# First stage of an attention and expert kernel rewritten as one list of 128 steps

## The chip, the cores and the metric

The kernel runs on one core of one Trainium2 chip. Its time is the device time of one launch in microseconds (us). The core has five engines that run their own instruction lists in order and meet only at semaphores: TensorE (PE, with PEld for its weight loads), VectorE (DVE), ScalarE (ACT), GpSimd (POOL) and SyncE (SP), which here only issues DMA transfers. ACT also issues a few transfers.

## What is computed

There are 16 batches of 128 rows by 256 columns in float32. Four residual blocks follow one another:

```
x = x + cross_attention_8_heads(layernorm(x), ctx, ctx)   # attention over the 256 columns, 16 rows a head
x = x + expert_choice_ffn(layernorm(x))                   # y = layernorm(x) @ expert_w + expert_b, router logits @ router_w + router_b
x = x + masked_cross_attention(layernorm(x), ctx)
x = x + top_half_ffn(layernorm(x))                        # 64 of 128 rows a batch through a gelu layer
```

The change touches the first stage, which does the first block and, of the second, the product `y` and the router's logits. For each of 16 batches and 8 heads it forms scores of 256 by 256, subtracts each row's maximum, exponentiates, multiplies by the values, divides, adds to `x`, normalizes and multiplies by `[expert_w | router_w]` (272 columns).

## The kernel before

**Steps.** One head of one batch is a step: 128 steps, numbered 8 b + (place of the head), 16 to a unit of two batches. A step has two products on PE. `scores` (L1089) gives the scores for the row maxima, which DVE takes with `maximum` (L527). `scores_t` (L1099) gives the transposed scores with the negated maxima added by two extra rows of the contraction; ACT exponentiates them (`exponential`, L891). Every fourth step `values` (L1112) multiplies four heads' probabilities by the values. `scores` runs 16 steps ahead of the exponentials at first and, catching up by two a step in steps 8 to 15, 24 ahead from step 16 on: there step t has `scores` and `maximum` number t + 24, `scores_t` number t + 2 and `exponential` number t. There are two banks for the scores and two for the transposed scores, so each producer may be two ahead of its consumer.

**Stacks.** Both products read a stack: the context and the normalized `x` of a unit, each as three bfloat16 parts (high, middle, low). For unit w the chain is: the unit is loaded (`load_stage`, L222); ACT makes the high part (`high_k`, L914), POOL the rest (`rest_k`, L334), ACT the middle (`mid_k`), POOL the low part (`low_k`, L339); DVE normalizes `x` (`stats_q`, `scale_q`) and `high_q`, `rest_q`, `mid_q`, `low_q` (L343 to 350) do the same for it; SP writes the six parts to DRAM (L233 to 243), issues the load of the next unit, waits for the parts and issues nine loads of the stack (`load_stacks`, L245). PE may start `scores` of unit w (step 12 for unit 2, step 16 w - 24 for later ones) once `stacks_loaded` has counted them. `mid_q` of unit 3 stands in step 13, of later units in step 16 w - 42 or 16 w - 44.

**Batch work.** After its eight steps a batch goes through `take_even` (ACT, L932: two products that pick the even heads), `gather_parts` (DVE, L539: two instructions of 256 columns), `invert` (reciprocal), `bring_over` (shuffle and product), `add_x1` (sum with `xs`, then the statistics), `root_rows` (POOL: inverse root), `scale_rows`, a transposition (PE), `take_xnt` (ACT), `yw` (PE, L1147) and `take_yw` (DVE, L576: bias added to `y` and to the logits). The row maxima of a batch are transposed (`max_t`), negated in two parts (`neg_high` on ACT, `neg_low` on DVE) and sent into the stack by two small DMAs (`send_neg_max`, L903).

**Order.** Each engine's order is written out by hand: a function `unit` for each engine with a place j for every piece, called once a unit, of which units 2 and 3 run in a hardware loop (`Fori`). On DVE `maximum` comes first in its step. On ACT `mid_k` stands right behind the first exponential of a unit. On POOL `rest_k` of the next stack is the last piece of a unit, behind `root_rows` of that unit's even batch; for the odd batch `root_rows` stands in the next unit.

After the stage come a softmax of the logits, a search of thresholds on DVE and PE, and a second pipeline over batch pairs that does the rest.

## Time and profile before

| what | value |
|---|---|
| three runs | 427.8, 426.61, 420.42 us; median 426.61 |
| profiled execution | 422.43 us, of which the span from first to last instruction 420.2 us |
| mean granted TensorE clock | 0.841 |
| busy, share of the span | PE 279.6 us (67%), DVE 317.7 (76%), ACT 167.6 (40%), POOL 94.8 (23%) |
| first exponential | 44.3 us from the start of the span |
| last exponential | starts at 237.5 us |
| first instruction of PE after the stage | 253.2 us |

The span begins with the first instruction. The stage ends at 253.2 us, where PE transposes the softmax of the logits; the remaining 167 us are the search and the second pipeline. A granted clock of 1.00 is TensorE at 2.4 GHz, and 0.5 is 1.2 GHz; values between are means over a stretch.

### The profile page before, as it was taken

To read this page: it belongs to the slowest core of one execution; us is meant where nothing else is said; L and a number is where in the kernel's file an instruction comes from. 1 tells how busy PE (TensorE), PEld (TensorE's weight loads), DVE (VectorE), ACT (ScalarE), POOL (GpSimd) and SP (SyncE) were. 2 spreads that over 40 slices of the span, in tenths; PEclk is the share of its full clock that TensorE was granted. 3 is DMA by queue.
4 is the path that set the end of the run, shared out by engine and by line. 5 is a ranking of instruction groups with operands and counts; after the bars stand their busy time and mean duration, and the time that the engine had idled before them with its cause. 6 is when DMAs were issued, how large, how long until landed. Compare 5 with 4: busy or idle time off the path is not lost.

```text
span 420.2 us, 7370 instructions
## 1 busy us (share of the span) xinstructions
PE 279.6 (67%) x1872; PEld 182.5 (43%) x1872; DVE 317.7 (76%) x989; ACT 167.6 (40%) x397; POOL 94.8 (23%) x222
## 2 busy tenths in 40 slices
PE   1134777777886877877778621001559999999996
PEld 0011333353442544444334310000438988888884
DVE  5847458899989889799986748888377888787631
ACT  4110543464654536464556500000111566445631
POOL 1101323352415224111111110000133322333200
PEclk9999975789698886899989965555555999999999
DMA  2789388959294581740000380000000000000001
GB/s 88 202 189 153 98 221 187 166 150 165 71 197 79 145 126 54 146 80 1 2 1 2 100 301 0 1 0 2 1 0 0 2 25 25 25 0 25 26 27 51
DMA packets 24379, 32.90 MB, mean 78 GB/s; under 512 B 4066, under 2 KB 22434, under 8 KB 22818
## 3 DMA queue, kind: packets, MB, share of 16 engines
q1 hardware_dynamic: 23842, 32.48, 33.5%
q10 hardware_dynamic: 512, 0.13, 0.2%
q8 instruction: 10, 0.16, 0.2%
q14 instruction: 15, 0.12, 0.1%
HBM read 24.02 MB, written 8.39 MB: 77 GB/s over the span
## 4 chain that ended last, share of the span: by engine, by line
DVE 35%; PE 33%; issue 12%; DMA 8%; ACT 4%; POOL 3%; SPq 2%; DVEq 1%; ACTq 1%; POOLq 0%
DVE row_max L531 7%; PE t_bank L1355 5%; PE pv_bank L1273 5%; PE pv_bank L1121 4%; DMA q_stack<-q_parts_dram 4%; DVE denom_inv L549 3%; PE score_bank L1094 3%; PE scoret_bank L1107 3%; PE t_bank L1150 2%; PE score_bank L1336 2%; DMA q_parts_dram<-q_parts 2%; ACT probs L895 2%; DMA q_stack<-neg_max 2%; PE score_bank L1303 2%; DVE junk L705 1%
## 5 line engine op out<-in xcount | busy, mean ns | idle before, releaser
L895 ACT ACTIVATE probs<-scoret_bank 128x512 f32<-128x512 f32 x128 | 73.1, 596 | 52.5 <-PE scoret_bank L1107 42.3
L531 DVE TENSOR_REDUCE row_max<-score_bank 128x2 f32<-128x512 f32 x112 | 74.4, 679 | 24.3 <-PE score_bank L1094 23.1
L1107 PE MATMUL scoret_bank<-q_stack,k_stack 98*128 98x256 bf16 (+1 forms) x256 | 54.6, 301 | 28.1 <-ACT probs L895 18.7
L1094 PE MATMUL score_bank<-k_stack,q_stack 96*128 96x256 bf16 (+1 forms) x240 | 53.6, 314 | 19.1 <-DMA q_stack<-q_parts_dram 11.0
L355 POOL TENSOR_SCALAR var_eps<-mv 128x1 f32<-128x1 f32 x48 | 9.2, 192 | 189.5 <-DVE mv L567 106.9
L1107 PEld LDWEIGHTS scoret_bank<-q_stack,k_stack 98*128 98x128 bf16 (+1 forms) x256 | 24.2, 104 | 46.6 <-ACT probs L895 20.5
L1121 PE MATMUL pv_bank<-probs,values_ones 128*32 128x256 f32 x512 | 42.0, 455 | 1.0 <-ACT probs L895 1.0
L1094 PEld LDWEIGHTS score_bank<-k_stack,q_stack 96*128 96x128 bf16 (+1 forms) x240 | 21.7, 105 | 47.8 <-issue 15.3
L1273 PE MATMUL pv_bank<-q_stack,k_stack 128*128 (+1 forms) x256 | 36.0, 285 | 0.4 <-ACT q_stack L1070 0.4
L1045 ACT COPY xnt<-score_bank 128x256 f32<-128x256 f32 x16 | 6.0, 373 | 74.6 <-PE score_bank L1294 74.6
L1273 PEld LDWEIGHTS pv_bank<-q_stack,k_stack 128*128 128x128 f32 x256 | 33.9, 202 | 1.3 <-issue 0.9
L1355 PE MATMUL t_bank<-k_stack,probs 128*128 128x256 f32 x128 | 29.4, 382 | 0.0
L357 POOL TENSOR_TENSOR rstd<-var_eps,minus_half 128x1 f32<-128x1 f32 x48 | 26.1, 543 | 8.8 <-POOL var_eps L355 8.8
L549 DVE RECIPROCAL denom_inv<-denom 128x256 f32<-128x256 f32 x16 | 27.7, 1732 | 0.0
L1355 PEld LDWEIGHTS t_bank<-k_stack,probs 128*128 128x128 f32 x128 | 23.7, 190 | 2.9
L1254 PE MATMUL t_bank<-count,same_expert 128*128 128x3 bf16 x15 | 2.8, 187 | 31.4 <-DVE equal L705 31.4
L1150 PE MATMUL t_bank<-wr_moving,xnt 128*128 128x272 f32 x64 | 22.0, 474 | 1.2 <-ACT xnt L943 1.2
L1064 ACT ACTIVATE probs<-pv_bank,b1s 128x128 f32<-128x128 f32 x64 | 17.6, 379 | 11.8 <-PE pv_bank L1273 11.7
L1121 PEld LDWEIGHTS pv_bank<-probs,values_ones 128*32 128x32 f32 x512 | 15.0, 122 | 16.2 <-issue 9.0
L1144 PE MATMUL t_bank<-ident,xn 128*128 128x128 f32 x32 | 7.0, 303 | 18.5 <-DVE xn L573 10.2
L1137 PE MATMUL t_bank<-ident,ctx_stage 128*128 128x128 f32 x32 | 7.6, 383 | 16.3 <-DMA x_stage<-in_x_dram 16.3
L1150 PEld LDWEIGHTS t_bank<-wr_moving,xnt 128*128 128x128 f32 x64 | 13.4, 234 | 8.1 <-issue 4.1
(182 smaller groups left out, 534.5 us busy)
## 6 DMA issues: line engine op xcount, KB each, us to landing
q_stack<-q_parts_dram SPq DMA_DIRECT2D x48, 128.0 KB, 6.9
k_parts_dram<-k_parts SPq DMA_DIRECT2D x24, 128.0 KB
q_parts_dram<-q_parts SPq DMA_DIRECT2D x24, 128.0 KB
k_stack<-k_parts_dram SPq DMA_DIRECT2D x8, 384.0 KB, 4.6
ctx_stage<-in_ctx_dram SPq DMA_DIRECT2D x8, 256.0 KB, 3.2
x_stage<-in_x_dram SPq DMA_DIRECT2D x8, 256.0 KB, 3.9
k_stack<-k_parts_dram SPq DMA_DIRECT2D x8, 256.0 KB, 5.3
xs<-in_x_dram SPq DMA_DIRECT2D x8, 256.0 KB, 7.3
```

The costliest lines, as they stand in the source:

```text
L355: pool.tensor_scalar(work, variance, EPS, factor, ALU.add, ALU.mult).then_inc(s[summed], 1)
L357: pool.tensor_tensor(dst, work, minus_half[:, 0:dst.shape[1]], ALU.pow).then_inc(s[ready], 1)
L531: dve.tensor_reduce(row_max[:, i, :, h], score_bank[bank_of][:, :].rearrange("p (m n) -> p m n", m=2), AX.X, ALU.max).then_inc(s["max_done ...
L549: dve.reciprocal(denom_inv[:, i, :], denom[:, i, :]).then_inc(s["div_step"], 1)
L895: act.activation(probs[:, j % PROBS, :], scoret_bank[j % 2][:, :], ACT.Exp).then_inc(s["exp_done"], 1)
L1064: act.activation(hid[:, h, :], hid_bank[h // 4][:, (h % 4) * P:(h % 4 + 1) * P], ACT.Gelu_apprx_tanh, bias=b1s[:, h:h + 1]).then_inc(s["f_ ...
L1094: ins = pe.matmul(to[:, m * D:(m + 1) * D], q_stack[0:QROWS, slot, h, b_in, m * P:(m + 1) * P], k_stack[0:QROWS, slot, h, b_in, :], start= ...
L1107: ins = pe.matmul(scoret_bank[j % 2][:, k * D:(k + 1) * D], k_stack[0:SROWS, slot, h, b_in, k * P:(k + 1) * P], q_stack[0:SROWS, slot, h, ...
L1121: ins = pe.matmul(pv_bank[i][pair * Q:(pair + 1) * Q, odd * D:(odd + 1) * D], values_ones[:, i, k, pair, odd, :], probs[:, (j - GROUP + 1 ...
L1150: ins = pe.matmul(t1_bank[:, 0:D + NE], xnt[:, i, k, :], wr_moving[:, k, :], start=(k == 0), stop=(k == 1))
L1273: ins = pe.matmul(hid_bank[h // 4][:, (h % 4) * P:(h % 4 + 1) * P], w1s[:, k, h * P:(h + 1) * P], zg[:, k, bass.ds(P * t, P)], start=(k == ...
L1355: ins = pe.matmul(y_bank[:, 0:D], hid[:, h, :], w2s[:, h, :], start=(h == 0), stop=(h == NF - 1))
```

## The change

The four `unit` functions and the loops go. Each engine runs one unrolled loop over t = 0 to 151, and tables say in which step each piece of a stack or of the maxima stands. `scores`, `scores_t` and `exponential` keep their places. The pieces of a batch b now stand at fixed steps: `values` 8b+7, `take_even` 8b+10, `gather_parts` 8b+11, `invert` 8b+12, `bring_over` 8b+13, `add_x1` 8b+14, `stats_x1` 8b+16, `root_rows` 8b+17, `scale_rows` 8b+18, transposition 8b+20, `take_xnt` 8b+21, `yw` 8b+22, `take_yw` 8b+24. `mid_k` stands three steps behind `high_k`.

Moved to other engines or merged: the sum `add_x1` goes from DVE to POOL; the statistics stay on DVE. The biases become three bfloat16 rows, made once on POOL (`split_bias`, ten small instructions), and are added by a third matmul in `yw`; `take_yw` is then one copy of 272 columns on ACT. `gather_parts` is one instruction of 512 columns. Some buffers of the second pipeline now lie in the stacks' memory, and `y` and `logits` share one tensor with rows of 272. The diff, cut to what is spoken of:

```
+def ahead(t):
+
+    if t < NH:
+        return [STEPS + t]
+    if t < STEPS:
+        return [2 * t + NH, 2 * t + NH + 1]
+    return [t + STEPS + NH] if t + STEPS + NH < LAST else []
...
+MAX_T = {1: 1, 2: 9, 3: 15, **{b: NH * b - 13 for b in range(4, NB)}}
+STAGE = {3: 9, 4: 21, **{w: STEPS * (w - 3) for w in range(5, NU)}}
+MID_K = {2: 0, 3: 11, 4: 23, **{w: STAGE[w] + 3 for w in range(5, NU)}}
+SCALE_Q = {2: 1, 3: 11, 4: 24, **{w: STAGE[w] + 6 for w in range(5, NU)}}
+HIGH_Q = {2: 3, 3: 13, 4: 25, **{w: STAGE[w] + 7 for w in range(5, NU)}}
+MID_Q = {2: 5, 3: 15, 4: 27, **{w: STAGE[w] + 9 for w in range(5, NU)}}
+CTX_T = {2: 5, 3: 12, 4: 23, **{w: STAGE[w] + 7 for w in range(5, NU)}}
+TAKE_VT = {2: 7, 3: 13, 4: 25, **{w: STAGE[w] + 9 for w in range(5, NU)}}
...
-        num_low = sb("num_low", [P, 2, D])
-        sum_high = sb("sum_high", [P, 2, D])
-        numer = sb("numer", [P, 2, D])
-        denom = sb("denom", [P, 2, D])
+        low_part = sb("low_part", [P, 2, 2, D])
+        gathered = sb("gathered", [P, 2, 2, D])
...
+            def add_x1(b, u, i, first):
+                wait_apart(pool, s["div_step"], 4 * b + 4)
+                wait_apart(pool, s["x_loaded"], 16 * (u + 1))
+                if not first:
+                    wait_apart(pool, s["xn_ready"], b - 1)
+                    wait_apart(pool, s["kept"], b - 1)
+                pool.tensor_tensor(x_new[:, i, :], gathered[:, i, 1, :], xs[:, b, :], ALU.add).then_inc(s["x1_done"], 1)
...
+                step(pool.tensor_copy(bias_terms[:, 0, :], bias_f[:, :]))
+                step(pool.tensor_tensor(bias_left[:, 0, :], bias_f[:, :], bias_terms[:, 0, :], ALU.subtract))
+                step(pool.tensor_copy(bias_terms[:, 1, :], bias_left[:, 0, :]))
+                step(pool.tensor_tensor(bias_left[:, 1, :], bias_left[:, 0, :], bias_terms[:, 1, :], ALU.subtract))
+                step(pool.tensor_copy(bias_terms[:, 2, :], bias_left[:, 1, :]))
+                for part in range(3):
+                    wait_apart(pool, s["ident_done"], 1)
+                    ins = pool.tensor_scalar(bias_kept[:, part, :], bias_terms[:, part, :], ident[0:3, part:part + 1], None, ALU.mult)
+                step(ins)
+                step(pool.tensor_tensor(bias_sum[:, :], bias_kept[:, 0, :], bias_kept[:, 1, :], ALU.add))
+                pool.tensor_tensor(bias_parts[:, :], bias_sum[:, :], bias_kept[:, 2, :], ALU.add).then_inc(s["bias_done"], 1)
...
+            for t in range(LAST + 3 * NH):
+                for b in range(NB):
+                    if t == NH * b + 17:
+                        root_rows(b, b % 2)
+                        keep_rows(x_new, b, b % 2)
+                for w in due(STAGE, t - 1):
+                    rest_k(w)
+                for w in due(STAGE, t - 2):
+                    root_q(w)
+                for w in due(MID_K, t - 1):
+                    low_k(w)
+                for w in due(HIGH_Q, t - 1):
+                    rest_q(w)
+                for w in due(MID_Q, t - 1):
+                    low_q(w)
+                for b in range(1, NB):
+                    if t == max(NH * b - 5, 2):
+                        fill_values(b, b // 2, b % 2, b < 2)
+                if t == NH + 1:
+                    split_bias()
+                for b in range(NB):
+                    if t == NH * b + 14:
+                        add_x1(b, b // 2, b % 2, b < 2)
...
                 dve.wait_ge(s["even_taken"], b + 1)
-                dve.scalar_tensor_tensor(denom[:, i, :], odd_heads, low[:, 0:1], sum_high[:, i, :],
+                if not (isinstance(b, int) and b < 2):
+                    dve.wait_ge(s["x1_done"], b - 1)
+                dve.scalar_tensor_tensor(gathered[:, i].rearrange("p k n -> p (k n)"), pv_bank[i][:, :], high[:, 0:1],
+                                         low_part[:, i].rearrange("p k n -> p (k n)"),
                                          ALU.mult, ALU.add).then_inc(s["div_step"], 1)
-                dve.scalar_tensor_tensor(numer[:, i, :], odd_heads, high[:, 0:1], num_low[:, i, :],
-                                         ALU.mult, ALU.add).then_inc(s["div_step"], 1)
 
...
+                                  ALU.mult).then_inc(s["div_step"], 1)
+
...
-                dve.tensor_tensor(y[:, b, :], t1_bank[:, 0:D], eb_rows[:, 0:D], ALU.add)
-                dve.tensor_tensor(logits[:, b, :], t1_bank[:, D:D + NE], eb_rows[:, D:D + NE], ALU.add).then_inc(s["yw_done"], 1)
...
+                    for b in range(NB):
+                        i = b % 2
+                        if t == NH * b + 16:
+                            stats_x1(b, i)
+                        if t == NH * b + 18:
+                            scale_rows(b, i, b < 2)
+                        if t == NH * b + 11:
+                            gather_parts(b, i)
+                        if t == NH * b + 12:
+                            invert(b, i)
+                        if t == NH * b + 13:
+                            bring_over(b, i)
+                    for w in due(STAGE, t if t < STEPS * 2 else t - 1):
+                        stats_q(w)
+                    for w in due(SCALE_Q, t):
+                        scale_q(w)
+                    for b in due(MAX_T, t - 2):
+                        neg_low(b, b % 2)
 
...
+            def take_yw(b):
+                act.wait_ge(s["yw_ready"], b + 1)
+                act.copy(y_ext[:, b, :], t1_bank[:, 0:D + NE]).then_inc(s["yw_done"], 1)
...
+                act.mul(low_part[:, i, 0, :], pv_bank[i][:, D:2 * D], low[:, 0:1])
+                act.mul(low_part[:, i, 1, :], pv_bank[i][:, 0:D], low[:, 0:1]).then_inc(s["even_taken"], 1)
...
+            for t in range(LAST + 3 * NH + 2):
+                if t < LAST:
+                    exponential(t // STEPS, t % STEPS, t < STEPS)
+                for b in range(NB):
+                    i = b % 2
+                    if t == NH * b + 24:
+                        take_yw(b)
+                    if t == NH * b + 10:
+                        take_even(b, i, b < 2)
+                    if t == NH * b + 21:
+                        take_xnt(b, i, b < 2)
+                for b in due(MAX_T, t - 1):
+                    neg_high(b, b // 2, b % 2)
+                for b in due(MAX_T, t - 3):
+                    send_neg_max(b // 2, b % 2)
+                for w in due(STAGE, t):
+                    high_k(w)
+                for w in due(MID_K, t):
+                    mid_k(w)
+                for w in due(HIGH_Q, t):
+                    high_q(w)
+                for w in due(TAKE_VT, t):
+                    take_vt(w)
+                for w in due(MID_Q, t):
+                    mid_q(w)
 
...
-                    ins = pe.matmul(t1_bank[:, 0:D + NE], xnt[:, i, k, :], wr_moving[:, k, :],
-                                    start=(k == 0), stop=(k == 1))
+                    pe.matmul(t1_bank[:, 0:D + NE], xnt[:, i, k, :], wr_moving[:, k, :],
+                              start=(k == 0), stop=False)
+                ins = pe.matmul(t1_bank[:, 0:D + NE], ones_bf[0:3, 0:P], bias_parts[:, :], start=False, stop=True)
...
+                for n in (ahead(t) if t < LAST else []):
+                    if n % STEPS == 0:
+                        pe.wait_ge(s["stacks_loaded"], 144 * (n // STEPS + 1))
+                    scores(score_bank[n % 2], n // STEPS, (n % STEPS) // NH, HEADS[n % NH], n - 1)
+                if t + 2 < LAST:
+                    scores_t(t + 2, (t + 2) // STEPS, (t + 2) % STEPS, True)
+                for b in due(MAX_T, t):
+                    pe.wait_ge(s["neg_done"], b)
+                    pe.wait_ge(s["vt_done"], before(CTX_T, t))
+                    max_t(b, b % 2)
+                for w in due(CTX_T, t):
+                    pe.wait_ge(s["neg_done"], before(MAX_T, t))
+                    ctx_t(w)
+                if t < LAST and t % GROUP == GROUP - 1:
+                    values(t, t // NH, t % STEPS, t < STEPS)
+                for b in range(NB):
+                    if t == NH * b + 20:
+                        if b > 0:
+                            pe.wait_ge(s["yw_done"], b)
+                        xn_t(b, b % 2)
+                    if t == NH * b + 22:
+                        if b == 0:
+                            pe.wait_ge(s["bias_done"], 1)
+                        yw(b, b % 2)
```

## Rows read from the trace of the kernel before

**Rows 1.** Busy time by stretch: start and end, length, engines, granted clock, DMA share, GB/s.
```profile
77.00:99.00 22.00, 17.36 (x140) 10.04 (x132) 19.20 (x41) 14.26 (x31) 7.79 (x13) 0.89 0.77 159
91.10:170.40 79.30, 60.85 (x444) 33.53 (x444) 71.20 (x145) 41.69 (x87) 25.97 (x49) 0.85 0.59 123
170.40:193.60 23.20, 18.18 (x146) 9.72 (x144) 20.42 (x42) 12.18 (x27) 3.17 (x11) 0.93 0.50 92
193.60:214.30 20.70, 15.38 (x141) 8.67 (x141) 19.31 (x41) 10.73 (x22) 2.38 (x8) 1.00 0.01 2
214.30:237.50 23.20, 17.40 (x148) 8.92 (x144) 16.72 (x40) 14.85 (x32) 4.15 (x12) 0.93 0.01 2
237.50:253.20 15.70, 5.50 (x28) 2.75 (x28) 8.55 (x30) 2.44 (x7) 2.16 (x6) 0.76 0.79 267
```

**Rows 2.** Who waited for whom between 99 and 180 us: total us, times, longest.
```profile
ACT k_parts L922 <- POOL k_rest L336: 10.7, 3, 3.8
```

**Rows 3.** Timeline around the start of unit 3: start, us, engine, line, operation, tiles, idle before.
```profile
127.86 1.15 POOL L336 TENSOR_TENSOR k_rest<-ctx_stage,k_parts 128x512 f32<-128x512 f32 x1
127.98 1.18 DVE L573 TENSOR_SCALAR xn<-x_new,mv,rstd 128x256 f32<-128x256 f32 x1
129.04 0.62 ACT L922 CAST k_parts<-k_rest 128x512 bf16<-128x512 f32 x1 [3.43 <-POOL k_rest L336]
```

**Rows 4.** Timeline of DVE and POOL, batch work in the last units.
```profile
207.61 0.46 DVE L542 SCALAR_TENSOR_TENSOR denom<-pv_bank,low,sum_high 128x256 f32<-128x256 f32 x1
208.39 0.67 DVE L531 TENSOR_REDUCE row_max<-score_bank 128x2 f32<-128x512 f32 x1
208.99 1.73 DVE L549 RECIPROCAL denom_inv<-denom 128x256 f32<-128x256 f32 x1
212.60 0.41 DVE L563 TENSOR_TENSOR x_new<-numer,xs 128x256 f32<-128x256 f32 x1
213.05 0.43 DVE L565 BATCH_NORM_STATS2 st<-x_new 128x6 f32<-128x256 f32 x1
214.01 0.19 POOL L355 TENSOR_SCALAR var_eps<-mv 128x1 f32<-128x1 f32 x1 [8.66 <-DVE mv L567]
214.88 0.40 POOL L366 COPY xs<-x_new 128x256 f32<-128x256 f32 x1
232.24 0.42 DVE L580 TENSOR_TENSOR y<-t_bank,eb_rows 128x256 f32<-128x256 f32 x1
232.66 0.47 DVE L542 SCALAR_TENSOR_TENSOR denom<-pv_bank,low,sum_high 128x256 f32<-128x256 f32 x1
```

**Rows 5.** Timeline of the chain that makes a stack: units 2 and 3, then 5.
```profile
51.16 1.16 POOL L350 TENSOR_TENSOR q_parts<-q_rest,q_parts 128x512 bf16<-128x512 f32 x1 [1.84 <-ACT q_parts L930]
...
66.67 0.62 ACT L930 CAST q_parts<-q_rest 128x512 bf16<-128x512 f32 x1
68.89 1.04 PE L1094 MATMUL score_bank<-k_stack,q_stack 96*128 96x256 bf16 x4 [2.15 <-DMA q_stack<-q_parts_dram]
69.61 1.29 DVE L531 TENSOR_REDUCE row_max<-score_bank 128x2 f32<-128x512 f32 x2 [1.61 <-PE score_bank L1094]
70.38 0.60 ACT L895 ACTIVATE probs<-scoret_bank 128x512 f32<-128x512 f32 x1 [3.10 <-PE scoret_bank L1107]
...
137.10 1.16 POOL L350 TENSOR_TENSOR q_parts<-q_rest,q_parts 128x512 bf16<-128x512 f32 x1 [1.57 <-ACT q_parts L930]
145.19 2.95 SPq L261 DMA_DIRECT2D q_stack<-q_parts_dram  x6
```

**Rows 6.** The page's list of DMA issues: KB each, median us from issue to landing.
```profile
q_stack<-q_parts_dram SPq DMA_DIRECT2D x48, 128.0 KB, 6.9
```

**Rows 7.** Timeline of ACT near the end of the stage, and its copy by line.
```profile
222.35 2.17 ACT L895 ACTIVATE probs<-scoret_bank 128x512 f32<-128x512 f32 x4 [2.13 <-PE scoret_bank L1107]
...
236.96 1.08 ACT L895 ACTIVATE probs<-scoret_bank 128x512 f32<-128x512 f32 x2 [1.74 <-PE scoret_bank L1107]
L943 ACT COPY xnt<-t_bank 128x256 f32<-128x256 f32 x16 | 5.6, 353 | 7.6 <-PE t_bank L1144 7.6
```

More of the change, by code:

```diff
@@ L38, with due, before @@
 PROBS = 2 * GROUP
-LEAD = NH
+LAST = STEPS * NU
+def ahead(t):
[12 more added lines that the diff above has]
+TAKE_VT = {2: 7, 3: 13, 4: 25, **{w: STAGE[w] + 9 for w in range(5, NU)}}
+def due(table, t):
+    return [n for n in sorted(table) if table[n] == t]
+def before(table, t):
+    return min(table) + sum(1 for n in table if table[n] < t)
 def build_program(nc, x, ctx_2048, mask, router_w, router_b, expert_w, expert_b,
@@ L304, in unit @@
                     load_stacks(u + 3, reused)
-            unit(0, True, True, False)
-            with sp.Fori(1, NU - 4) as u:
-                unit(u, True, True, True)
-            unit(NU - 4, False, True, True)
-            unit(NU - 3, False, False, True)
-            unit(NU - 2, False, False, True)
+            for u in range(NU - 1):
+                unit(u, u < NU - 4, u < NU - 3, u > 0)
             sp.wait_ge(s["scorest_ready"], STEPS * NU)
@@ L381, in _ @@
             root_q(2)
-            low_k(2)
-            rest_q(2)
-            low_q(2)
-            def unit(u, first, second, parts, more_parts, last):
-                if second:
-                    rest_k(u + 3)
-                    root_q(u + 3)
-                if parts and not first:
-                    low_k(u + 3)
-                    rest_q(u + 3)
-                fill_values(2 * u + 1, u, 1, first)
-                if parts and not first:
-                    low_q(u + 3)
-                if not first:
-                    root_rows(2 * u - 1, 1)
-                    keep_rows(x_new, 2 * u - 1, 1)
-                if first:
-                    rest_k(u + 3)
-                    root_q(u + 3)
-                if not last:
-                    fill_values(2 * u + 2, u + 1, 0, False)
-                if first:
-                    low_k(u + 3)
-                    rest_q(u + 3)
-                    low_q(u + 3)
-                root_rows(2 * u, 0)
-                keep_rows(x_new, 2 * u, 0)
-                if more_parts and not first:
-                    rest_k(u + 4)
-                    root_q(u + 4)
@@ L992, in unit @@
-            def unit(u, second, last, parts, more_parts):
-                for j in range(STEPS):
-                    exponential(u, j, False)
-                    if j == 1:
-                        take_even(2 * u - 1, 1, second)
-                    if j == 1 and second:
-                        high_k(u + 3)
-                    if j == 2 and not last:
-                        neg_high(2 * u + 2, u + 1, 0)
-                    if j == 3 and not last:
-                        send_neg_max(u + 1, 0)
-                    if j == (3 if second else 0) and parts:
-                        mid_k(u + 3)
-                    if j == 2:
-                        take_xnt(2 * u - 2, 0, second)
-                    if j == (4 if second else 2) and parts:
-                        high_q(u + 3)
-                    if j == (6 if second else 4) and parts:
-                        mid_q(u + 3)
-                    if j == 6 and parts:
-                        take_vt(u + 3)
-                    if j == 9:
-                        take_even(2 * u, 0, False)
-                    if j == 10 and not last:
-                        neg_high(2 * u + 3, u + 1, 1)
-                    if j == 11 and not last:
-                        send_neg_max(u + 1, 1)
-                    if j == 10:
-                        take_xnt(2 * u - 1, 1, second)
-                    if j == 13 and more_parts:
-                        high_k(u + 4)
```

284 lines of the change are left out of this document (47 added, 237 removed).

## The prediction

> **What bounds the kernel now.** I read first the totals: DVE is the busiest engine (317.7 us), yet 76% is a mean over unlike parts, so it proves little. The table of busy time by stretch comes next, with cuts where DVE starts the maximum of steps 48, 96 and 112, ends the last one, where the last exponential starts, and where the stage ends at 253.2 us [rows 1]. The reader is to see three regimes. From 193.6 to 214.3 us DVE is busy 19.31 of 20.7 us at a granted clock of 1.00: 16 steps bound by DVE. From 91.1 to 170.4 us the same 16 steps take 26.4 us (79.3 over 3), though DVE's work is only 23.7 a stretch: something else stops it. After 214.3 us there are no maxima, and a chain through all engines sets the pace.
>
> The waits name the something: ACT's `mid_k` stood 3 times for `rest_k` of POOL, 10.7 us together [rows 2]. The timeline shows how: ACT idles 3.43 us with 15 exponentials queued behind it, while POOL, which had stood behind an inverse root, makes `rest_k` from 127.86 us on, and a DVE instruction that normally takes 0.41 us takes 1.18 beside it [rows 3].
>
> **DVE's work.** Start to start, the sum costs 0.45 us (212.60 to 213.05), the two bias additions 0.42 (232.24 to 232.66), the two gathers 0.78 (207.61 to 208.39) [rows 4]. The merged gather of 512 columns is not in the trace: at least the 0.60 of a maximum over 512 columns in the same memory (208.39 to 208.99), at most the two halves, 0.78. I take the middle, 0.69, as it has one more operand than the maximum. So 0.45 + 0.42 + 0.09 = 0.96 us go for each batch, 1.9 us per 16 steps. A stretch with no new stack falls from 20.7 to 18.8 us. One with a stack took 22.0 where little stalled (77 to 99 us [rows 1]); less 1.9 that is 20.1.
>
> **What is added elsewhere.** POOL's sum: between the 0.40 us of a 256-column copy [rows 4] and the 1.15 of a 512-column subtraction [rows 3], and I take 0.58, half the latter, as it reads two inputs. POOL was busy 26.0 of 79.3 us, so 1.2 us a stretch lie beside DVE; they matter only through what queues behind: `low_q` and `root_rows`. ACT's copy of 272 columns is 0.37 us by the 353 ns of the 256-column one [rows 7]; ACT is busy 41.7 of 79.3 us and it costs nothing but once at the end. The third matmul of `yw` is at most a half of a score's pair, which takes 1.04 us for four at half clock [rows 5], so 0.26 us; PE has 20.7 - 15.4 us to spare. The ten bias instructions on POOL stand at step 9, in a pause where it waits for unit 3's data; if each cost 0.4 to 1.15 us and the cover went, that would be 4 to 11 us of delay for `rest_k` of unit 3. I take none, since unit 3 is late for another reason, next.
>
> **The chain that takes the stall's place.** What is late next is the stack itself. From the end of POOL's `low_q` (52.32) to PE's first product from stack 2 (68.89) it was 16.6 us; for stack 5 from 138.26 to the last issue at about 147.6, and 6.9 us to land, 16.3 [rows 5, 6]. Below 16 nothing excludes a gain but the queue's order is unchanged; above, more overlap with other transfers may cost. I take 17, with 16 and 20 as ends. The diff moves `mid_q` of unit 3 from step 13 to step 15, and this crosses a barrier: exponential 13 ran before stack 2 had landed, but exponential 14 starts at 70.38, after it [rows 5], since step 12 of PE needs stack 2. Worked out for stack 3: stack 2 lands at 69.4, half a microsecond later than before because its own `mid_q` moves one step; DVE's first two maxima end at 71.3; the reciprocal, now in step 12 behind them, ends at 73.0 (1.73 less overlap [rows 4]); two maxima, then shuffle and product end at 75.1; POOL's sum stands ahead of `low_q` and ends at 76.0; `low_q` ends at 77.1. Before, `mid_q` was at 66.67 [rows 5] and `low_q` ended by 68.6. So stack 3 lands at 77.1 + 17 = 94.1 and the maximum of step 48 starts at 94.8 (0.72 us later, as 68.89 to 69.61 [rows 5]), 3.7 us behind the 91.1 of before.
>
> For stack 4, `scale_q` stands in the very step that waits for stack 3, then `high_q`, `rest_q`, `mid_q`, `low_q`: about 5.9 us, so step 64 comes 5.9 + 17 = 22.9 us later, at 117.7. For later stacks `low_q` follows stack w by 0.72 (product) + 0.6 (maximum) + 0.96 (statistics to POOL, 213.05 to 214.01) + 1.27 (inverse root and copy, 214.01 to 215.28) [rows 4] + 1.15 (itself) = 4.7 us. The loop's period is 21.7 us, against 20.1 of DVE. With DVE's small waits and collisions I take 22 for each of the next three.
>
> **The sum.** Step 112's maximum: 117.7 + 3 x 22 = 183.7 (193.6 before). Last one: + 18.8 = 202.5 (214.3). Last exponential: 24 steps at (236.96 - 222.35) / 16 = 0.91 us [rows 7], 21.9 us, so 224.4 (237.5). End of the stage: the 15.7 us of before and 0.5 for the two new hand-overs and the third matmul: 240.6 (253.2). Gain 12.6 us; the second pipeline keeps its length. Against the profiled execution, 422.4 - 12.6 = 409.8; its time lies 1% under the median of 426.6, from which I get **414.0**.
>
> **The rivals.** *The stack is never late.* If the loads come sooner, or DVE's other work hides them, step 48 stays at 91.1, four stretches of 20.1 follow, then 18.8, 21.9 and 16.2: 228.4, a gain of 24.8, **401.8**. For it: the list of waits shows none of PE for a stack after the one of 68.89 [rows 5]. Against: `mid_q` of unit w had 18 to 20 steps to spare, and has 13 to 15 now, 16.3 to 18.8 us at the new pace of 20.1 / 16.
>
> *The chain is longer.* At 20 us step 48 comes at 97.8, step 64 25.9 later, and three periods of 24.7 end at 197.8; with 18.8, 21.9 and 16.2 the stage ends at 254.7: **428**, no change. For it: unit 5's issues on SP fill 9.9 of its 16.3 us (138.26 to 148.14 [rows 5]), and the next unit's load goes ahead of the stack's.
>
> *POOL blocks DVE.* The 1.18 in place of 0.41 us [rows 3] is a DVE instruction that ended with POOL's, not after its own time. Should each of 16 sums stop DVE for its whole 0.58, 9.3 us are lost: **423**. The Trainium skill (SBUF — State Buffer, section "SBUF: two separate sides") says that a POOL instruction and a DVE one with two SBUF inputs or in a two-port mode exclude each other for a whole instruction; by it, moving work from DVE to POOL may return nothing, which is this case; the trace agrees where the two meet. Against: in the step of the sum DVE mostly reduces scores, and in rows 3 the meeting was with an instruction twice as long.
>
> *Slower: TensorE's clock.* PE's work in a stretch with a stack is 60.85 / 3 x 0.85 = 17.2 us at full clock [rows 1]. If PE, stopped at step 16w - 24 by each late stack, mostly runs at 1.2 GHz, it becomes the bound. It decides from a mean granted clock of 0.70, where 17.2 / 0.70 = 24.6 us undo the gain. At 0.65 four stretches of 26.5 from 94.8, then 23.7, 21.9 and 16.2 end at 262.6: **436**. For it: the stretches with stalls have 0.85, the ones without 0.93 to 1.00. Against: the stalls of 3.43 us vanish, the new ones are about 1 to 3 us. The Trainium skill (TensorE: Matmul & The Clock Gate, section "HAM oscillation — how this bites in real kernels") says that PE slows down again at each wait for data; by that the late stacks would cost twice.
>
> **How the numbers follow.** Chances: forecast 0.50, stack never late 0.20, longer chain 0.15, POOL blocks 0.07, clock 0.08. About 2% (8.5 us, so below 418.1) is what can be told from no change here. Faster: nine tenths of the forecast and the first rival, 0.65. Slower: 0.08. Within: the rest, 0.27. The range runs from 398 (the first rival with a few microseconds more) to 426 (most of the second); it leaves out the clock, half of the longer chain and the ends of the runs' own spread of 7 us.
>
> **What would show it.** Right: no ACT wait of `mid_k` for POOL; PE waits for the DMA of a stack at step 24 (some 6 us) and again at step 40 (1 to 3); 21 to 23 us from the maximum of step 64 to that of 80; no DVE instruction reading the product of `yw`; last exponential near 224 and stage end near 241. Wrong: the maximum of step 48 at 91 or before, stretches of 20 us, or a granted clock under 0.8 from 95 to 200 us. A second pipeline that changes its length would break the sum as well.

## Result: 6.95% slower, and the profile after

The kernel after took **453.57 us** (median of four runs, 452.29 to 454.3), the kernel before 425.75 (420.42 to 427.8). The ratio is 1.0695, with a 95% interval from 1.0591 to 1.0799. The profiled execution took 453.62 us, of which its span is 451.8. I had predicted 414.0, with a range from 398 to 426.

The page of the kernel after, its busy line and four groups (busy us, mean ns of one, idle time before, releaser):

```profile
PE 293.6 (65%) x1888; PEld 185.2 (41%) x1888; DVE 298.2 (66%) x925; ACT 170.7 (38%) x413; POOL 113.1 (25%) x248
...
L574 DVE TENSOR_REDUCE row_max<-score_bank 128x2 f32<-128x512 f32 x112 | 73.5, 675 | 65.0 <-PE score_bank L1027 64.6
L875 ACT ACTIVATE probs<-scoret_bank 128x512 f32<-128x512 f32 x128 | 74.2, 600 | 77.0 <-issue 50.8
...
L404 POOL TENSOR_TENSOR x_new<-gathered,xs 128x256 f32<-128x256 f32 x16 | 11.6, 722 | 73.4 <-DVE gathered L599 68.4
...
L586 DVE SCALAR_TENSOR_TENSOR gathered<-pv_bank,high,low_part 128x512 f32<-128x512 f32 x16 | 11.9, 742 | 6.3 <-ACT low_part L921 6.3
```

DVE lost the work it was meant to lose: 317.7 us before, 298.2 now. The maxima cost the same, yet DVE now waits 64.6 us for PE's scores ahead of them; the page of before has this for the same group:

```profile
L531 DVE TENSOR_REDUCE row_max<-score_bank 128x2 f32<-128x512 f32 x112 | 74.4, 679 | 24.3 <-PE score_bank L1094 23.1
L895 ACT ACTIVATE probs<-scoret_bank 128x512 f32<-128x512 f32 x128 | 73.1, 596 | 52.5 <-PE scoret_bank L1107 42.3
```

The exponentials changed what they wait for: PE before, "issue" (50.8 us) now, which means that ACT's own queue was held up by something that is no busy instruction. Busy time of the kernel after by stretch of sixteen exponentials (numbers 38, 54, 70, 86 and 102 start about at the cuts) is to be read beside [rows 1]:

```profile
126.00:154.40 28.40, 21.86 (x147) 11.13 (x145) 19.43 (x41) 13.98 (x31) 10.04 (x18) 0.76 0.53 112
154.40:182.00 27.60, 21.07 (x151) 10.87 (x150) 20.15 (x41) 14.28 (x32) 10.04 (x18) 0.81 0.55 116
182.00:209.00 27.00, 19.92 (x150) 10.64 (x150) 19.60 (x37) 13.34 (x30) 7.00 (x14) 0.87 0.46 98
209.00:235.00 26.00, 20.05 (x143) 10.63 (x144) 17.84 (x34) 11.18 (x26) 4.74 (x12) 0.80 0.05 12
```

The last row is the telling one. DMA is busy 5% there: no stack is made, and [rows 1] had 16 such steps in 20.7 us, bound by DVE. Now DVE is busy 17.84 of 26 us. So the loss comes also where no stack is made. The waits of 90 to 250 us (total, times, longest):

```profile
ACT probs L875 <- issue: 45.3, 11, 5.1
DVE row_max L574 <- PE score_bank L1027: 44.1, 16, 4.8
PE scoret_bank L1040 <- ACT probs L875: 36.8, 26, 2.9
```

ACT is held 11 times in some 11.5 batches, 4.1 us each. The timeline shows by what (ACTq is ACT issuing DMAs):

```profile
208.45 1.74 DVE L592 RECIPROCAL denom_inv<-gathered 128x256 f32<-128x256 f32 x1
208.56 0.60 ACT L875 ACTIVATE probs<-scoret_bank 128x512 f32<-128x512 f32 x1
...
210.66 0.43 DVE L596 STREAM_SHUFFLE denom_own<-denom_inv 128x256 f32<-128x256 f32 x1
...
211.13 0.42 DVE L599 TENSOR_TENSOR gathered<-gathered,denom_own 128x256 f32<-128x256 f32 x1
...
211.48 0.40 DVE L579 SCALAR_TENSOR_TENSOR neg_max<-t_bank,neg_max 8x256 bf16<-8x256 f32 x1
...
211.91 1.29 ACTq L886 DMA_DIRECT2D q_stack<-neg_max  x2
...
213.25 1.08 ACT L875 ACTIVATE probs<-scoret_bank 128x512 f32<-128x512 f32 x2 [4.09 <-issue]
213.90 0.39 PE L1040 MATMUL scoret_bank<-q_stack,k_stack 98*128 98x256 bf16 x2 [2.71 <-ACT probs L875]
...
215.23 0.60 PE L1027 MATMUL score_bank<-k_stack,q_stack 96*128 96x256 bf16 x2
...
215.94 0.69 DVE L574 TENSOR_REDUCE row_max<-score_bank 128x2 f32<-128x512 f32 x1 [2.86 <-PE score_bank L1027]
```

Read it from 211.48. `neg_low` starts there, the last piece of its step on DVE, behind the reciprocal, the shuffle and the product. ACT's last exponential ended at 209.16; the next piece in its queue is `send_neg_max`, which needs `neg_low`. It issues its two DMAs at 211.91, and the next exponential, whose input had long been in its bank, starts at 213.25. PE stood for the free bank until 213.90, did `values` (1.07 us) before the next scores, and DVE ran dry until 215.94. The same rows stand 14 us later, and so on: a loop DVE, ACT, PE, DVE, closed once a batch. In the kernel before `neg_low` stood right behind the maximum:

```profile
207.28 0.40 DVE L536 SCALAR_TENSOR_TENSOR neg_max<-t_bank,neg_max 8x256 bf16<-8x256 f32 x1
...
207.71 1.36 ACTq L906 DMA_DIRECT2D q_stack<-neg_max  x2
...
209.17 2.17 ACT L895 ACTIVATE probs<-scoret_bank 128x512 f32<-128x512 f32 x4 [1.60 <-PE pv_bank L1121]
```

It is ahead of the two gathers and the reciprocal [rows 4], and ACT hardly waits. In the list `neg_low` of batch b is at step 8b - 11, which is the step of another batch's `bring_over`, and stands behind it.

### The profile page after: what moved, and what is told of

It reads as the page before. It is cut to its first block, busy times and chain, and to the rows that moved or that the text cites. A ratio compares the mean times of both kernels' runs of the same rounds, so it can differ in the third digit from the quotient of the medians.

```text
span 451.8 us, 6847 instructions
## 1 busy us (share of the span) xinstructions
PE 293.6 (65%) x1888; PEld 185.2 (41%) x1888; DVE 298.2 (66%) x925; ACT 170.7 (38%) x413; POOL 113.1 (25%) x248
## 4 chain that ended last, share of the span: by engine, by line
DVE 33%; PE 33%; issue 11%; DMA 8%; ACT 5%; ACTq 4%; POOL 4%; SPq 2%; DVEq 1%; POOLq 0%
PE pv_bank L1054 7%; DVE row_max L574 6%; DVE denom_inv L592 5%; PE scoret_bank L1040 4%; ACTq L886 4%; DMA q_stack<-q_parts_dram 4%; PE t_bank L1237 4%; PE score_bank L1027 4%; PE pv_bank L1155 3%; ACT probs L875 2%; DMA q_parts_dram<-q_parts 2%; PE score_bank L1218 2%; POOL rstd L390 2%; DVE junk L685 1%; DVE denom_own L596 1%
## 5 line engine op out<-in xcount | busy, mean ns | idle before, releaser
L574 DVE TENSOR_REDUCE row_max<-score_bank 128x2 f32<-128x512 f32 x112 | 73.5, 675 | 65.0 <-PE score_bank L1027 64.6
L875 ACT ACTIVATE probs<-scoret_bank 128x512 f32<-128x512 f32 x128 | 74.2, 600 | 77.0 <-issue 50.8
L1040 PE MATMUL scoret_bank<-q_stack,k_stack 98*128 98x256 bf16 x256 | 61.1, 332 | 53.4 <-ACT probs L875 44.5
L1027 PE MATMUL score_bank<-k_stack,q_stack 96*128 96x256 bf16 x240 | 57.7, 337 | 23.3 <-DMA q_stack<-q_parts_dram 16.1
L1040 PEld LDWEIGHTS scoret_bank<-q_stack,k_stack 98*128 98x128 bf16 x256 | 24.8, 114 | 75.7 <-ACT probs L875 57.6
L1054 PE MATMUL pv_bank<-probs,values_ones 128*32 128x256 f32 x512 | 48.6, 514 | 0.0
L1027 PEld LDWEIGHTS score_bank<-k_stack,q_stack 96*128 96x128 bf16 x240 | 21.4, 114 | 56.5 <-DVE row_max L574 21.5
L404 POOL TENSOR_TENSOR x_new<-gathered,xs 128x256 f32<-128x256 f32 x16 | 11.6, 722 | 73.4 <-DVE gathered L599 68.4
L390 POOL TENSOR_TENSOR rstd<-var_eps,minus_half 128x1 f32<-128x1 f32 x48 | 26.3, 549 | 9.1 <-POOL var_eps L388 9.1
L592 DVE RECIPROCAL denom_inv<-gathered 128x256 f32<-128x256 f32 x16 | 27.9, 1744 | 0.1
L1054 PEld LDWEIGHTS pv_bank<-probs,values_ones 128*32 128x32 f32 x512 | 16.3, 133 | 19.2 <-issue 15.0
L1083 PE MATMUL t_bank<-wr_moving,xnt 128*128 128x272 f32 x64 | 18.6, 415 | 1.2 <-ACT xnt L927 1.2
L1070 PE MATMUL t_bank<-ident,ctx_stage 128*128 128x128 f32 x32 | 7.2, 367 | 16.2 <-DMA x_stage<-in_x_dram 16.2
L586 DVE SCALAR_TENSOR_TENSOR gathered<-pv_bank,high,low_part 128x512 f32<-128x512 f32 x16 | 11.9, 742 | 6.3 <-ACT low_part L921 6.3
```

Of the source, the lines that this page charges most:

```text
L390: pool.tensor_tensor(dst, work, minus_half[:, 0:dst.shape[1]], ALU.pow).then_inc(s[ready], 1)
L574: dve.tensor_reduce(row_max[:, i, :, h], score_bank[bank_of][:, :].rearrange("p (m n) -> p m n", m=2), AX.X, ALU.max).then_inc(s["max_done ...
L592: dve.reciprocal(denom_inv[:, i, :], gathered[:, i, 0, :]).then_inc(s["div_step"], 1)
L875: act.activation(probs[:, j % PROBS, :], scoret_bank[j % 2][:, :], ACT.Exp).then_inc(s["exp_done"], 1)
L1027: ins = pe.matmul(to[:, m * D:(m + 1) * D], q_stack[0:QROWS, slot, h, b_in, m * P:(m + 1) * P], k_stack[0:QROWS, slot, h, b_in, :], start= ...
L1040: ins = pe.matmul(scoret_bank[j % 2][:, k * D:(k + 1) * D], k_stack[0:SROWS, slot, h, b_in, k * P:(k + 1) * P], q_stack[0:SROWS, slot, h, ...
```

## Experiments

Theory at the outset: the place of `neg_low`. Rivals: the later pieces of the stacks; TensorE's lower clock; the work moved to POOL and ACT. The code shows the edits shortened. Ratios are to runs of the kernel before on the same chip (medians 420.74 to 422.83).

**1. Only `neg_low` moved, in the kernel after:** one step earlier and ahead of the batch pieces.

```
  # DVE, step t, behind the maximum
+    for b in due(MAX_T, t - 1):
+        if b >= 4: neg_low(b, b % 2)
  # last in the step
     for b in due(MAX_T, t - 2):
-        neg_low(b, b % 2)
+        if b < 4: neg_low(b, b % 2)
```

> The kernel after with one piece moved: for batches from 4 on, DVE's neg_low stands one step earlier, ahead of that step's statistics, reciprocal, shuffle and product instead of behind them. Theory A (order on DVE): in the kernel after, ACT's send of the maxima waits for neg_low, which queues behind a 1.66 us reciprocal, two maxima and 0.8 us of shuffle and product; ACT is stopped 4.0 us and issues for 1.3 us at each batch, and PE and then DVE run dry for 2.9 to 3.5 us. Moving it 3 us forward takes about 3 us off each of 12 batches: 415 to 422 us in place of 453.6, ACT's idle time in front of an exponential that follows a send falls from 33 us (8 times between 130 and 250 us) to under 12. Theory B (the chain of the stacks, period 4.7 + 17 us, has become the bound): no gain beyond 3 us, and PE waits for a stack's transfer grow. Theory C (TensorE at 1.2 GHz is the bound): under 5 us of gain.

Measured: 419.91 us, ratio 0.9953 (0.991 to 0.9995), against 1.0695. By the medians that is 34 us less than the kernel after, from one instruction of 0.40 us at another place. Its timeline, then its stretches (in the last two POOL makes no parts of a stack, in the last nothing is moved either):

```profile
186.96 0.40 DVE L579 SCALAR_TENSOR_TENSOR neg_max<-t_bank,neg_max 8x256 bf16<-8x256 f32 x1
187.06 0.60 ACT L879 ACTIVATE probs<-scoret_bank 128x512 f32<-128x512 f32 x1
...
187.29 1.73 DVE L592 RECIPROCAL denom_inv<-gathered 128x256 f32<-128x256 f32 x1
187.39 1.29 ACTq L890 DMA_DIRECT2D q_stack<-neg_max  x2
...
188.73 1.09 ACT L879 ACTIVATE probs<-scoret_bank 128x512 f32<-128x512 f32 x2 [1.07 <-PE scoret_bank L1044]
```
```profile
132.00:155.90 23.90, 18.68 (x151) 10.09 (x150) 21.50 (x41) 14.29 (x33) 10.06 (x18) 0.93 0.62 131
155.90:179.70 23.80, 18.56 (x151) 10.08 (x150) 21.28 (x41) 14.26 (x32) 10.07 (x18) 0.93 0.64 117
179.70:198.70 19.00, 16.58 (x149) 9.04 (x147) 18.34 (x35) 11.96 (x27) 4.77 (x12) 1.00 0.58 107
198.70:216.80 18.10, 14.28 (x132) 7.66 (x131) 16.09 (x32) 11.99 (x27) 4.77 (x12) 1.00 0.01 2
```

The reciprocal now lies beside the two DMA issues. The clock rises too: 0.93 where stacks are made against 0.76 to 0.87, 1.00 in the last stretch against 0.80. The lower clock of the kernel after came with its stops and went with them; how many of the 34 us it carried itself no run separates.

**2. The consumer moved instead:** ACT's `send_neg_max` two steps later, `neg_low` left last.

```
-for b in due(MAX_T, t - 3):
+for b in range(1, NB):
+    if t == MAX_T[b] + (3 if b < 4 else 5):
         send_neg_max(b // 2, b % 2)
```

> The kernel after with ACT's send of the negated maxima two steps later (for batches from 4 on), DVE's order untouched. Theory A (ACT's wait for DVE, not the DMA issue itself, costs): ACT reaches the send when neg_low is done, the exponentials of the next two steps run ahead, and the time falls to 415 to 430 us; the transfer has 6 steps left until PE needs it. If what costs were the 1.3 us that ACT spends on two issues, nothing would change: 450 to 455. Theory B (stacks) and C (clock): within 5 us of 453.6.

Measured: 426.85 us, ratio 1.0104 (1.0021 to 1.0187), 27 us less than the kernel after. So it isn't the time at which `neg_low` runs that costs, but what queues behind the instruction that waits for it. What keeps this kernel 7 us above experiment 1 stays open.

**3. Rival, the stacks:** their pieces back at about the steps of before, `neg_low` left last.

```
-STAGE = {3: 9, 4: 21, **{w: STEPS * (w - 3) ...}}
+STAGE = {3: 8, 4: 17, **{w: STEPS * (w - 3) - 3 ...}}
-SCALE_Q = {2: 1, 3: 11, 4: 24, **{w: STAGE[w] + 6 ...}}     # MID_K, HIGH_Q likewise
+SCALE_Q = {2: 1, 3: 10, 4: 19, **{w: STAGE[w] + 4 ...}}
-MID_Q = {2: 5, 3: 15, 4: 27, **{w: STAGE[w] + 9 ...}}
+MID_Q = {2: 5, 3: 13, 4: 23, **{w: STAGE[w] + 7 ...}}
```

> The kernel after with the stack pieces (high_k, mid_k, stats_q, scale_q, high_q, mid_q and with them POOL's four) moved back to about the steps of the kernel before, so that mid_q has 20 steps to the first product instead of 15 (17 instead of 13 for stack 4, 11 instead of 9 for stack 3). Theory B (the late stack sets the period of 28 us): gain of 10 us or more. Theory A: PE's waits for stacks vanish, but the gain is under 5 us but for the first stacks (stack 3 lands at 97.7 and stack 4 at 125.7 us: up to 8 us there), 445 to 453 us in all.

Measured: 460.42 us, ratio 1.0906 (1.0826 to 1.0986): slower still, where I had expected 445 to 453. The rival falls: here stacks 5 to 7 landed 18 to 21 us before their first maxima, in the kernel after 6.7 to 7.7 us before, so in neither were they what was late. The timeline of its first unit shows a new stall:

```profile
65.36 2.85 POOL L425 TENSOR_SCALAR bias_kept<-bias_terms,ident 3x272 bf16<-3x272 bf16 x3 [0.24 <-POOL bias_terms L422]
...
70.97 1.56 DVE L530 TENSOR_SCALAR qn<-x_stage,mv,rstd_q 128x256 f32<-128x256 f32 x2 [6.88 <-POOL rstd_q L390]
...
76.07 0.62 ACT L910 CAST q_parts<-qn 128x512 bf16<-128x512 f32 x1 [11.65 <-issue]
```

With the data of unit 3 wanted sooner, the ten bias instructions stand in front of its inverse root on POOL, DVE stops in its queue for it, and ACT's send, which waits for DVE, holds ACT for 11.65 us. This is the same mechanism with a longer cause, but it is not why the kernel is slower than the one after: the maximum of step 48 comes 1.7 us later there, that of step 64 0.7 us. The rest is lost behind it, where steps 64 to 112 take 88.8 us in place of 82.2; why stays open.

**4. The loss put into the kernel before:** `neg_low` behind `bring_over` two steps later, the send two later; nothing else of the change. (Two pieces that share a bank with the maxima, the context's transposition on PE and a copy on ACT, move by two steps and one.)

```
-if j == 2 and scored and not first:  neg_low(2 * u + 2, 0)
+if j == 4 and scored and not first:  neg_low(2 * u + 2, 0)    # last in the step
...
-if j == 3 and not last:              # ACT, the send
+if j == 5 and not last:
```

> The kernel before with the suspected order put in: from unit 1 on neg_low stands behind shuffle and product, two steps later, and ACT's send two steps later with it (the transposition of the context on PE and its copy also move 2 and 1 steps, since they share a bank). Nothing else of the change. Theory A: ACT now stops at each send for DVE's reciprocal, shuffle and product, 2 to 3 us for 12 to 13 batches: 440 to 455 us against 425.8. Theories B and C, and a loss due to work moved to POOL and ACT: within 5 us of before.

Measured: 449.02 us, ratio 1.0677 (1.0591 to 1.0764), against 1.0695 for the whole change. The old kernel gets the new one's rows:

```profile
205.09 0.40 DVE L536 SCALAR_TENSOR_TENSOR neg_max<-t_bank,neg_max 8x256 bf16<-8x256 f32 x1
...
205.53 1.36 ACTq L906 DMA_DIRECT2D q_stack<-neg_max  x2
206.94 1.09 ACT L895 ACTIVATE probs<-scoret_bank 128x512 f32<-128x512 f32 x2 [4.88 <-issue]
...
207.59 0.61 PE L1107 MATMUL scoret_bank<-q_stack,k_stack 98*128 98x256 bf16 x2 [2.78 <-ACT probs L895]
```

**5 to 7. What is left of the change's gain.** With experiment 1 as base, first earlier places for the stacks' pieces were tried, many (5) and `scale_q` of units 5 to 7 alone (6), then the sum was put back on DVE (7).

```
-SCALE_Q = {..., **{w: STAGE[w] + 6 ...}}   # 5 and 6
+SCALE_Q = {..., **{w: STAGE[w] + 3 ...}}
-MID_Q   = {..., 3: 15, 4: 27, ... + 9}     # 5 only, with STAGE[4] 19 for 21, HIGH_Q two earlier
+MID_Q   = {..., 3: 13, 4: 25, ... + 7}
```

> The kernel of e1_low_early with more pieces moved: DVE's scale_q of units 5 to 7 three steps earlier (ahead of the reciprocal), high_q and mid_q two steps earlier, mid_q of unit 3 in step 13 again with the transposition and the copy of its context one step or none earlier, and the pieces of unit 4 one to two steps earlier. Theory: what is left of the loss is the same pattern (high_q of ACT stands 2.8 us for scale_q behind DVE's reciprocal, once a unit: stretches of 23.9 us in place of 20 to 21), and the late stack 3 (low_q ends at 78.7 us, 7 us after what it could). Expected 400 to 408 us. Rival (the stack's chain of 17 us plus 4.7 holds the period at 22): 410 to 416. Rival (clock): no gain.

> The kernel of e1_low_early with scale_q of units 5 to 7 alone three steps earlier on DVE, ahead of gather and reciprocal. Theory (same pattern of order): ACT's wait of high_q for DVE (2.8 us, 3 such units) goes, 4 to 9 us less than e1_low_early, 411 to 416 us. Rival (stack chain is the bound): the time goes into PE's waits for the stack's transfer, under 3 us of gain.

> The kernel of e1_low_early with the sum of a batch back on DVE (in step 8b+16, ahead of the statistics) and no sum on POOL. Theory (moving work off DVE is worth its start-to-start time where DVE is the bound): 0.45 us for each of the batches in stretches bound by DVE, 2 to 5 us slower than e1_low_early. Rival (POOL's sum, measured 0.72 us, blocks DVE or delays low_q by as much as it saves): equal or faster than e1_low_early.

Measured: 416.55 us, ratio 0.9841 (0.9742 to 0.9941), where I had expected 400 to 408; then 417.77, ratio 0.989 (0.9793 to 0.9987), expected 411 to 416; then 421.73, ratio 0.9994 (0.9951 to 1.0037). In the first of them stack 3 landed at 88.5 us in place of 96.3, and exponential 32 started at 108.4 in place of 108.1. Bringing the stack forward by 8 us was worth nothing there; the second unit was held by ACT's queue again:

```profile
87.33 0.60 ACT L879 ACTIVATE probs<-scoret_bank 128x512 f32<-128x512 f32 x1 [2.92 <-issue]
...
91.43 0.69 DVE L574 TENSOR_REDUCE row_max<-score_bank 128x2 f32<-128x512 f32 x1 [3.20 <-PE score_bank L1031]
```

The sum on POOL is worth about 2 us by the medians, and the intervals of 1 and 7 overlap, so its worth isn't told from nothing.

**8 and 9. More room between steps.** In the kernel before, `mid_k` of ACT two steps later, against the stall of [rows 2]; and, in the kernel of experiment 5, the send, `mid_k` and unit 4's `high_q` and `mid_q` one step later each, and the transposition of batch 3's maxima one step earlier.

```
-if j == (3 if second else 0) and parts:   # 8: mid_k in the kernel before
+if j == (3 if second else 2) and parts:
-for b in due(MAX_T, t - 3):               # 9: the send
+for b in range(1, NB):
+    if t == MAX_T[b] + (3 if b < 4 else 4):
         send_neg_max(b // 2, b % 2)
```

> The kernel before with ACT's mid_k two steps later in units 2 to 4, nothing else. If the stall of 3.4 to 3.8 us that I read at the head of units 2 to 4 was what made these stretches 26.4 us long, it shrinks by one to two us each and the time falls by 3 to 8 us. If it was hidden by another limit (DVE or the chain behind mid_k), within 2 us of before.

> The kernel of e5_low_and_scale_early with one more step between the waits that are left: the send of the maxima one step later from batch 4 on, mid_k one step later from unit 5 on (it stood 2.0 us for POOL), high_q and mid_q of unit 4 one step later (high_q stood 2.9 us for DVE), the maxima of batch 3 one step earlier. Theory (what is left are ACT's waits of 1 to 3 us on pieces one step behind DVE or POOL): 2 to 6 us less than e5_low_and_scale_early, 410 to 415 us. Rival (DVE's own work of 20 to 22 us a stretch is the bound there): within 2 us of it.

Measured: 421.54 us, ratio 0.9989 (0.9941 to 1.0038), and 418.93, ratio 0.9934 (0.9889 to 0.9979). Neither gains on its base, where the theories had 3 to 8 us for the first and 410 to 415 us for the second: two more misses. In the first the wait of `mid_k` is gone, and in its place:

```profile
131.20 0.37 ACT L901 ACTIVATE neg_max<-t_bank 8x256 bf16<-8x256 f32 x1 [1.90 <-PE t_bank L1130]
...
133.91 0.62 ACT L926 CAST q_parts<-qn 128x512 bf16<-128x512 f32 x1 [1.57 <-DVE qn L487]
```

Taking away the stall of 3.43 us in [rows 3] by itself bought nothing that shows.

**10. One move of the change, in the kernel before:** `take_yw` as two copies on ACT. The bias is left out of `y` and the logits here.

```
+act.copy(y[:, b, :], t1_bank[:, 0:D])
+act.copy(logits[:, b, :], t1_bank[:, D:D + NE])     # ACT, j = 7 and 13
-take_yw(2 * u - 2)                                  # DVE, j = 8 and 14
```

> The kernel before with the two reads of the product of yw taken from DVE to ACT as two copies (the bias is left out of y and of the logits). One part of the change alone. By its price on DVE (0.42 us a batch where DVE is the bound, 6 to 9 of 16 batches) 2 to 6 us faster than before. If ACT's queue makes the copy late and PE's next transposition waits for it: within 2 us, or slower.

Measured: 410.06 us, ratio 0.9765 (0.9679 to 0.9852). The two additions cost DVE 0.42 us a batch [rows 4], some 7 us in all, and leaving them out gained 12, where I had expected 2 to 6. What queued behind them can be seen in the trace: PE's transposition waits for the bank that they read. PE's waits of 77 to 210 us in the kernel before, and then here:

```profile
PE t_bank L1144 <- DVE logits L581: 5.9, 5, 1.4
PE t_bank L1144 <- DVE xn L573: 5.0, 5, 1.2
```
```profile
PE t_bank L1149 <- DVE xn L573: 2.9, 5, 0.9
```

With the additions gone, `xn` also starts ahead of POOL's `k_rest` and not behind its start, and takes 0.41 us and not 1.18 [rows 3]. How the 12 us divide between these no run separates.

```profile
125.10 0.41 DVE L573 TENSOR_SCALAR xn<-x_new,mv,rstd 128x256 f32<-128x256 f32 x1
125.29 1.23 POOL L336 TENSOR_TENSOR k_rest<-ctx_stage,k_parts 128x512 f32<-128x512 f32 x1
```

**11. All moves but the sum, in the old order.** This is the whole computation.

```
+split_bias()                                   # POOL, first unit
+pe.matmul(t1_bank[:, 0:D + NE], ones_bf[0:3, 0:P], bias_parts, start=False, stop=True)
+one gather of 512 columns for the two of 256   # DVE
+take_yw as in 10                               # ACT
```

> The kernel before in its own order of steps (neg_low right behind the maximum, the send and the stack pieces where they were), with all of the change's moves but one: expert and router bias as a third accumulating product on TensorE (its three parts split on GpSimd during the first unit), y and the logits taken out by ScalarE, gathering as one 512-column instruction on VectorE; the sum x_new stays on VectorE. Theory that the moves were good and the list's place for neg_low ate them: 405 to 410 us; the run with the copies on ScalarE alone took 410.1, and the merged gathering takes 2 x 0.78 - 0.74 = 0.8 us off VectorE per batch, of which at most some 10 us can show and 2 to 4 us should, since VectorE waits elsewhere for part of it. Rival: the split on GpSimd (some 7 us of it) makes the second unit late and gives this back: 412 to 416 us. Rival that the list was needed to use these moves: 420 us or more.

Measured: **412.67 us, ratio 0.9737 (0.9683 to 0.979)**: faster than both kernels, 9% under the kernel after, though not the 405 to 410 I expected. The merged gather and the bias on PE add nothing that shows to experiment 10. The expectation had priced the merging wrong: the 0.78 us are what the two gathers take together (207.61 to 208.39 in [rows 4]), not each, and the merged one takes 0.68 from start to start, so 0.1 us goes for each batch and not 0.8. The moves are those of experiment 7, whose ratio is 0.9994, but for the copies out of `yw` (two here, one there); the order differs.

## Why the prediction was wrong

**The failed step** is the pace of 16 steps in *The sum*: 22 us with a stack and 18.8 without. It was made of DVE's busy time and the stacks' landing, and the wait of ACT's send for `neg_low`, twice in 16 steps, stood in it at nothing without a reason; *What is added elsewhere* said of ACT that more work costs nothing there but at the end. Measured in the kernel after were 26.3 to 28.3 us from step 64 to 112 and 23.1 from there to the last maximum, with ACT held 4.1 us at each batch. `neg_low` and the send stand one step apart in the list. But from the start of the reciprocal to that of `neg_low` DVE needs 3.0 us (208.45 to 211.48), and ACT, at 0.6 us an exponential, is at its send long before. None of my four rivals had this wait, and none went beyond 436 us for 453.57. I had looked for what is late between units and not for what repeats in each batch. Experiments 1 and 2 remove the loss from either end (34 and 27 us), and experiment 4 makes it alone (28 us by the medians): shown.

**The rest of the sum** can be read from experiment 1, which is the predicted kernel without that wait. Starts of the maxima, in us:

| | predicted | experiment 1 | after |
|---|---|---|---|
| step 48 | 94.8 | 96.8 | 101.4 |
| step 64 | 117.7 | 122.1 | 133.7 |
| step 112 | 183.7 | 191.7 | 215.9 |
| last | 202.5 | 209.9 | 239.0 |
| last exponential | 224.4 | 231.4 | 266.1 |
| end of the stage | 240.6 | 249.4 | 284.1 |

Of the 8.8 us between prediction and experiment, 2.0 are there at step 48 and 2.4 come up to step 64; the next two periods took 23.9 us each, not 22 (3.7 together), and the third 21.9; the last two stretches were right within 0.6 (18.2 for 18.8, 21.5 for 21.9); the end took 18.0, not 16.2. In the longer periods stands the same pattern once a unit, `high_q` of ACT behind DVE's `scale_q` (experiment 1, 90 to 250 us):

```profile
ACT q_parts L914 <- DVE qn L530: 12.8, 4, 4.5
```

Experiment 6 moved that piece in three units and gained 2 us by the medians, which the intervals don't tell from nothing. After the stage the kernels keep their length (451.8 - 284.1 = 167.7 us; before 420.2 - 253.2 = 167.0), as predicted.

**Sizes.** The merged gather, 0.69 predicted, takes 0.742, and 0.68 from start to start. POOL's sum takes 0.722 us, not 0.58.

**The stack chain.** I made it the bound from step 48 on. Its length was right: from the end of `low_q` to the landing it took 16.3 to 18.8 us in experiment 1, and 16.5 to 18.2 before. (One reading under it was not: the 16.3 us of before, put together from the last issue and a median, belong to unit 6 and not 5, whose stack landed at 156.2, 17.9 us behind 138.26; and of the 9.9 us on SP there at most 6.8 are issues, the rest is waiting.) In experiment 1 it did set step 48, by a little:

```profile
71.03 1.04 PE L1031 MATMUL score_bank<-k_stack,q_stack 96*128 96x256 bf16 x4 [5.27 <-DMA q_stack<-q_parts_dram]
...
96.34 0.39 PE L1031 MATMUL score_bank<-k_stack,q_stack 96*128 96x256 bf16 x2 [1.31 <-DMA q_stack<-q_parts_dram]
```

Of the 2.0 us by which step 48 came late there, 1.6 are there at the first product from stack 2 (71.03, 69.4 predicted). No later stack held it, but for one weight load by 0.4 us. In the kernel after, stack 3 landed at 97.7 us and its first maximum started only at 101.4: the stack was there and PE was not, and PE waited for the DMA of none from stack 3 on. Experiments 3 and 5 show that bringing stacks forward bought nothing or little. The sign that no `mid_k` would wait for POOL failed too; it still waits, half as long as in [rows 2] (90 to 250 us):

```profile
ACT k_parts L906 <- POOL k_rest L369: 5.5, 3, 1.8
```

**The rivals.** *The stack is never late* holds in the kernel after from stack 3 on, but it had no term for the loss. *The chain is longer* put it at 20 us, and it stayed at 16.3 to 18.8. *POOL blocks DVE*: experiment 7 puts the sum back and is 2 us slower by the medians, within the noise, where this rival would have gained. That DVE's normalizing instructions are stretched beside POOL's is in the trace: one takes 0.41 us where POOL makes at most a copy beside it (206.24 in the kernel after), a pair of the same shape 0.73 (7.19 in the kernel before), and such a pair 1.60 us in experiment 5, beside a POOL instruction of 1.19:

```profile
139.05 1.60 DVE L530 TENSOR_SCALAR qn<-x_stage,mv,rstd_q 128x256 f32<-128x256 f32 x2
139.31 1.19 POOL L374 TENSOR_TENSOR k_parts<-k_rest,k_parts 128x512 bf16<-128x512 f32 x1
```

The sum itself mostly meets maxima: in the kernel after, the one at 212.03 us lay beside a pair of maxima that took 1.27 us, no more than other pairs. Three of the 16 lay beside a normalizing instruction, which took 0.49 us and not 0.40. *The clock*: I gave "slower" only this way. The granted clock did fall, to 0.76 to 0.87 in the stretches with stacks, but not to the 0.70 from which the rival decides, and PE was busy 20 to 22 of 26 to 28 us, so it was not the bound; experiment 1 brought the clock back by moving one DVE instruction. The Trainium skill (TensorE: Matmul & The Clock Gate, "HAM oscillation — how this bites in real kernels") says of a kernel in which PE waits for data at every tile that it slows down again each time; the trace agrees, with a granted clock of 0.76 to 0.87 with the stops and 0.93 to 1.00 without them.

**What stays open.** Experiments 7 and 11 have the same pieces and differ by 9 us of median. In the first, exponentials 16 to 32 take 32.0 us (77.4 to 109.4), in the second 22.0 (77.0 to 99.0); from there to the last exponential the list is the faster of the two, by 2.8 us (109.4 to 234.5, 125.1 us, against 99.0 to 226.9, 127.9). So the list loses these 10 us in one unit alone. DVE waits 8.9 us for PE's scores in it in experiment 7 and 2.4 us in experiment 11, and in experiment 7 ACT stands in it for unit 4's `scale_q`, which it doesn't in experiment 11:

```profile
100.32 0.62 ACT L916 CAST q_parts<-qn 128x512 bf16<-128x512 f32 x1 [3.76 <-DVE qn L527]
```

Which of its places there is to blame wasn't found: an earlier stack 3 and an earlier `scale_q` of unit 4, and with it a later send and an earlier transposition of one batch's maxima, left exponential 32 at 108.4 and 109.7 (experiments 5 and 9).

## What to carry to other kernels

Before pricing a new order, write down for each wait on an in-order engine what stands ahead of the awaited instruction on its own engine, and what stands behind the waiting one. Here 0.40 us of work behind 2.6 us of unrelated batch work cost 34 us, because the reader's queue held the exponentials and these held PE. A distance in steps is no slack if the two engines run through a step at different paces. And price a removed instruction by its readers too: leaving out 7 us of additions gave 12.

## What the hardware showed

- Issuing two small DMAs from ACT's queue takes 1.29 to 1.5 us (the first pair of a run 1.9 to 2.0), and no instruction behind them in the queue starts in it; with the wait ahead it makes the 4.1 us a batch. Work that stands ahead of them still runs beside the issue: in experiment 2 an exponential starts at 121.99 and a copy at 122.48 us, beside issues at 121.58 and 122.24.
- POOL's sum of 256 columns from two inputs takes 722 ns, its copy of 256 columns 0.40 us [rows 4]; a tensor-scalar instruction on three rows of 272 columns took 950 ns (experiment 3, 2.85 us for three).
